# Layer scores as 64x64 products on the band of keys that each half block of queries sees

## The reference

```
h = shift_token(x);  q, k, v = split(h @ wqkv)         # 8 heads of 64
q, k = rotary_xpos(l2norm(q) * qs, l2norm(k) * ks)
# blocks of 128 queries, which see their own block of keys and the one before it
sim = q . k   masked where  i < j  or  i > j + 128
x = x + (softmax(sim) @ v) @ wo
h = layernorm(shift_token(x));  a, g = split(h @ w1 + b1)
x = x + (a * gelu(g)) @ w2 + b2
```

## Time and profile before

| | us |
|---|---|
| median of 3 runs | 1422.95 |
| lowest and highest run | 1420.28, 1424.81 |
| the profiled execution's own time | 1424.29 |
| its span, first to last instruction | 1422.5 |

### The profile page before, as it was taken

How to read it: one execution, slowest core, us unless ns; L and a number is a source line. 1 busy time by engine, 2 the same in 40 slices (tenths; PEclk the granted TensorE clock), 3 DMA queues, 4 the chain that set the end, 5 groups by cost and what they waited for, 6 DMA issues and landing times.

```text
span 1422.5 us, 24115 instructions
## 1 busy us (share of the span) xinstructions
PE 1374.8 (97%) x7740; PEld 1050.5 (74%) x7740; DVE 963.8 (68%) x2671; ACT 878.1 (62%) x2223; POOL 762.1 (54%) x522
## 2 busy tenths in 40 slices
PE   6999997999999999999999999999999999999988
PEld 5878775777777777777777777786777777777756
DVE  6877765767676666666667777676767676766657
ACT  4556656575747575747475766666565757575763
POOL 2425765564647373738373747464655646473710
PEclk9999999999999999999999999999999999999998
DMA  7111100000000000000001010000000000000046
GB/s 220 38 51 60 55 30 1 1 1 0 0 0 0 0 0 0 0 0 0 0 1 60 14 47 1 1 0 0 0 0 0 0 0 0 0 0 0 0 145 210
DMA packets 35243, 33.33 MB, mean 23 GB/s; under 512 B 8364, under 2 KB 32896, under 8 KB 35200
## 3 DMA queue, kind: packets, MB, share of 16 engines
q1 hardware_dynamic: 35200, 32.79, 7.3%
HBM read 24.39 MB, written 8.39 MB: 23 GB/s over the span
## 4 chain that ended last, share of the span: by engine, by line
PE 78%; ACT 11%; DVE 5%; issue 4%; POOL 1%; DMA 0%; ACTq 0%; SPq 0%; DVEq 0%; POOLq 0%
PE l_psF L1399 9%; PE l_psP L842 9%; PE l_ring L842 9%; PE l_ring L1399 8%; PE l_ring L1469 7%; ACT l_att L1073 7%; PE l_psP L1453 6%; PE l_psF L1487 6%; PE l_psS L1410 5%; PE l_psS L1422 4%; PE l_ring L653 3%; PE l_psF L1439 2%; PE l_psS L671 1%; PE l_psP L688 1%; ACT L1163 1%
## 5 line engine op out<-in xcount | busy, mean ns | idle before, releaser
L955 POOL TENSOR_TENSOR l_att<-l_att 128x1024 f32<-128x1024 f32 x64 | 153.1, 2403 | 315.7 <-DVE l_att L880 315.7
L1007 POOL TENSOR_TENSOR l_att<-l_att,l_rinv 128x1024 f32<-128x1024 f32 x64 | 126.4, 1975 | 70.7 <-DVE l_rinv L1243 70.4
L1053 ACT ACTIVATE l_att<-l_psP 128x384 f32<-128x384 f32 (+1 forms) x128 | 70.3, 549 | 120.7 <-PE l_psP L1453 120.4
L1248 DVE COPY l_att<-l_psP 128x384 f32<-128x384 f32 (+1 forms) x128 | 78.9, 617 | 86.7 <-PE l_psP L1453 82.5
L1453 PE MATMUL l_psP<-ident,l_att 128*128 128x128 f32 x896 | 124.5, 279 | 2.0 <-DVE l_att L1248 1.5
L1453 PEld LDWEIGHTS l_psP<-ident,l_att 128*128 128x128 f32 x896 | 98.6, 141 | 32.4 <-issue 28.2
L962 POOL TENSOR_TENSOR l_att<-l_att,l_rn 128x1024 f32<-128x1024 f32 x64 | 120.8, 1910 | 0.7 <-ACT l_rn L861 0.5
L1073 ACT ACTIVATE l_att<-l_psF,l_nb 128x256 f32<-128x256 f32 x256 | 118.1, 483 | 2.1 <-DVE l_nb L1236 2.1
L971 POOL TENSOR_TENSOR l_u_lo<-l_att,l_u_hi 128x512 fp32r<-128x512 f32 x75 | 95.7, 1288 | 39.1 <-ACT l_u_hi L1048 39.0
L1469 PE MATMUL l_ring<-l_att 128*64 128x256 f32 (+1 forms) x1024 | 112.5, 362 | 2.0 <-ACT l_att L1053 1.4
L1236 DVE CUSTOM_DVE_ANT_0 l_psF<-l_psF,w_mask 128x256 f32<-128x256 f32 x256 | 101.1, 456 | 16.3 <-issue 16.3
(11 more groups left out here) (209 smaller groups left out, 4037.2 us busy)
## 6 DMA issues: line engine op xcount, KB each, us to landing
a_tables<-in_x SPq DMA_DIRECT2D x8, 512.0 KB, 4.3
scratch_s<-a_o SPq DMA_DIRECT2D x8, 512.0 KB, 3.2
l_att<-in_x SPq DMA_DIRECT2D x8, 512.0 KB, 8.8
l_att<-scratch_s SPq DMA_DIRECT2D x8, 512.0 KB, 9.0
out_dram<-l_att SPq DMA_DIRECT2D x7, 512.0 KB, 7.8
aw_stage<-in_wqkv SPq DMA_DIRECT2D x2, 768.0 KB, 5.9
l_att<-in_wqkv SPq DMA_DIRECT2D x2, 768.0 KB, 5.4
w_w_raw<-in_w SPq DMA_DIRECT2D x2, 640.0 KB
```

The source lines that it names most:

```text
L955: pool.tensor_tensor(rot[:, t, :], rot[:, t, :], t2[t % 2], ALU.add).then_inc(S["added"], 1)
L1007: pool.tensor_tensor(pr, pr, along(inv, 2 * P), ALU.mult).then_inc(S["p_done"], 1)
```

## The change

`scores` makes of each product of 128 queries and 256 keys two products of 64 queries and 192 keys (`part` 0 and 1, whose results go to partitions 0 to 63 and 64 to 127). The four products of a block (two heads, two halves) use the four 64x64 quarters of the array. The first block of all has 128 keys for both halves. In the steps with both halves, unit 1 keeps the two products of its first block whole (`scores(i, 1, 1)`).

The waits of `scores` become a function of their own, `score_operands`. In the steps with both halves it is called with `ahead` from the group that comes before the scores: from `hidden`'s last tile ahead of the last product (and, because the loop passes there twice, also ahead of its low part), from `down` ahead of the last product of the four tiles (for unit 2) and of the fifth tile (for unit 3), and from `p_transposes` of units 0 to 3 ahead of the last transpose (for units 4 to 7). In the first step the waits stay in front of the scores.

```diff
+BAND = P // 2
...
-        def hidden(i, j, attn, parts=("hi", "lo")):
+        def hidden(i, j, attn, parts=("hi", "lo"), ahead=None):
...
                     for n, (k, w, a) in enumerate(terms):
+                        if ahead is not None and n == 3 * KD - 1:
+                            score_operands(i, ahead)
...
-        def down(i, c, tiles):
+        def down(i, c, tiles, ahead=None):
...
                 for m, (w, u) in enumerate(((W.w2_hi, U_hi), (W.w2_hi, U_lo), (W.w2_lo, U_hi))):
+                    if ahead is not None and k == tiles[-1] and m == 2:
+                        score_operands(i, ahead)
...
-        def scores(i, u, tiles=0):
+        def score_operands(i, u, tiles=TT):
+
+            if u < 2:
+                ge(pe, S["qT_sb"], TT * i + tiles)
+                ge(pe, S["kT_sb"], TT * i + tiles)
+            else:
+                ge(pe, S["exp_done"], UNITS * i + u - 1)
+
+        def scores(i, u, whole=0):
+
             pair, half = u // 2, u % 2
-            if u == 0 or tiles:
-                ge(pe, S["qT_sb"], TT * i + (tiles or TT))
-                ge(pe, S["kT_sb"], TT * i + (tiles or TT))
-            if u >= 2:
-                ge(pe, S["exp_done"], UNITS * i + u - 1)
             ps = scores_of[u % 2]
             for tt in range(2):
                 t = half * 2 + tt
-                c0 = 0 if t else P
                 for par in range(2):
                     rows = slice(par * DH, (par + 1) * DH)
-                    last = pe.matmul(ps[:, par * 512 + tt * 2 * P + c0:par * 512 + (tt + 1) * 2 * P], QT[rows, pair, t * P:(t + 1) * P],
-                                     KT[rows, pair, max(t - 1, 0) * P:(t + 1) * P], start=True, stop=True, skip_group_check=True)
+                    c = par * 512 + tt * 2 * P - (t - 1) * P
+                    for part in range(1 if tt < whole else 2):
+                        n = P if tt < whole else BAND
+                        q = t * P + part * BAND
+                        k0, k1 = (q - P, q + n) if t else (0, P)
+                        last = pe.matmul(ps[part * BAND:part * BAND + n, c + k0:c + k1], QT[rows, pair, q:q + n], KT[rows, pair, k0:k1],
+                                         start=True, stop=True, skip_group_check=True)
...
-        def p_transposes(i, u):
+        def p_transposes(i, u, ahead=None):
...
                     for own in (range(2) if u % 2 or tt else (1,)):
+                        if ahead is not None and par and tt and own:
+                            score_operands(i, ahead)
...
-                    hidden(i, j, attn)
+                    hidden(i, j, attn, ahead=0 if attn and j == HT - 1 else None)
...
-                    scores(i, 0, TT - 1)
+                    score_operands(i, 0, TT - 1)
+                    scores(i, 0)
...
             if attn and ffn:
                 scores(i, 0)
                 ge(pe, S["u_done"], HT * (i - 1) + HFULL)
+                scores(i, 1, 1)
+            elif attn:
+                score_operands(i, 1)
                 scores(i, 1)
-            elif attn:
-                scores(i, 1, TT)
...
-                down(i, 0, range(0, 4))
+                down(i, 0, range(0, 4), ahead=2 if attn else None)
...
                     if u < UNITS:
+                        if not ffn:
+                            score_operands(i, u)
                         scores(i, u)
                     if ffn and u in (2, 4):
-                        down(i, 0, range(3 + u // 2, 4 + u // 2))
+                        down(i, 0, range(3 + u // 2, 4 + u // 2), ahead=u + 1 if u == 2 else None)
...
                     if u >= 3:
-                        p_transposes(i, u - 3)
+                        p_transposes(i, u - 3, u + 1 if ffn and u + 1 < UNITS else None)
```

## The result

The changed kernel takes 1427.13 us (median of 14 runs, 1425.41 to 1429.21). The kernel before takes 1422.59 us beside it (14 runs, 1420.28 to 1425.93). The ratio is 1.0031, with a 95% interval of 1.0023 to 1.0040: slower by about 0.3%. The forecast was 1425.2 us and a ratio of about 1.0016, with 1423 to 1430 as its own range. So the direction is as forecast, and the size is about twice the forecast's. The profiled execution has a span of 1426.2 us (1422.5 before).

A forecast was written before the change was run, and what follows sets the result against it. TensorE is busy 97%, but the scores stretch was taken as bound by a chain of ScalarE's exponentials, last transposes, copies and values. 15 x 0.18 - 0.5 = +2.2 us on 1422.95 gave 1425.2 us, range 1423 to 1430.

The forecast's parts named there:

- four side by side at the quarter rate: Scores units: four quarter products run at once, 0.41 ns a column; psF 0.26 us and psS 0.16 us shorter.
- Rival B: Scores products: the four don't run side by side; +3.3 us an iteration, 1472 us; chance 0.10.
- the estimate by the Trainium skill: Scores units: issue costs some 62 ns a matmul, 1.14 us a unit, +1.5 us an iteration, 1445 us; chance 0.03.
- the moved wait holds the last product, and through it both copies: Unit 4's wait in unit 0's transposes: the last transpose waits, and ScalarE's copy starts 0.41 us later.
- Rival A: Moved waits hold nothing back and the shorter units count: -0.59 us an iteration, 1413.6 us; chance 0.17.
- nothing is gained by moving them: Entries to the scores: moved waits shorten no entry, gain taken as 0; ends 0 and 0.20 us at six entries.
- the last term: After unit 3's transposes: VectorE's copy takes 0.66 us, values group starts at 682.77 instead of 682.59; +0.18 us an iteration.
- no scores product lies on the chain that is left: Chain from unit 2's exponentials to the last values group: it holds no scores product; the iteration grows by 0.18 us.
- shorter scores only fill waits: Steps with both halves: the shorter scores products give nothing on the chain; the iteration grows by 0.18 us.
- First step: Attention half alone, no moved waits: shorter units give 0 to 1.7 us, taken as 0.5 us less.
- "Same": Whole kernel: time within 0.3%, 4.3 us, of the kernel before; chance 0.55.
- "slower": Whole kernel: slower by more than 0.3%, from above +0.29 us an iteration; chance 0.28.

The follow-up runs named there:

- e2: The changed kernel with its waits moved but the scores products as before the change: ratio 1.0066 to the kernel before.
- e5: The changed kernel with the waits of units 5 to 7 back in front of their scores, unit 4's still ahead of the last transpose: ratio 0.9974 to before.
- e6: The changed kernel with the waits of units 4 to 6 back in front of their scores, unit 7's still ahead of the last transpose: ratio 0.9985 to before.
- e9: e1 with the waits on the scores products themselves and TensorE's loop over the steps written out: ratio 0.9956 to the kernel before.
- e1: The changed kernel with quarter products kept and all waits back in front of the scores, on instructions of their own: ratio 0.9956 to the kernel before.
- e10: e8 with the waits on the scores products themselves and TensorE's loop written out: 1413.33 us, ratio 0.9937 to the kernel before.
- e8: e1 with the sixth second-layer tile placed after unit 0's transposes, before scores 4, instead of after scores 4: 1413.25 us, ratio 0.9926 to the kernel before.
- e13: The kernel before, whole scores products, with only the sixth second-layer tile moved behind unit 0's transposes: ratio 0.9993 to the kernel before.

## Why the forecast was right in kind and small in size

Step by step, from scores 0, forecast against the changed kernel's step 6:

| | forecast | measured |
|---|---|---|
| psF unit, psS unit | 0.81, 0.70 | 0.81, 0.71 |
| first `down` product | 1.80 | 1.83 |
| scores 2, 3 | 4.96, 6.79 | 4.97, 6.79 |
| ScalarE's copy of unit 0 | 8.84 | 8.83 |
| scores 4, 5 | 8.73, 11.47 | 8.72, 11.45 |
| values after scores 5 | 12.32 | 12.36 |
| scores 6, 7 | 14.79, 17.53 | 14.82, 17.56 |
| VectorE's last copy | 17.64 | 17.67 |
| values after scores 7 | 18.35 | 18.51 |
| growth of the period | 0.18 | 0.33 |

**Right: four side by side at the quarter rate.** Within a psF unit the trace has the products start in fours, 7 ns apart (673.100, .107, .113, .120), and each four 0.162 us after the one before. These are 768 columns in one of the two passes, so two passes cost 0.42 ns a column; I had taken 0.41. Rival B falls. So does the estimate by the Trainium skill (TensorE: Matmul & The Clock Gate, "Wait — 56ns, not 53.3ns?"): four instructions in 0.162 us are 41 ns each, less than its 62. (The prediction's 1.14 us for such a unit is also added up too low: 16 x 0.062 and its fixed part of 0.18 are 1.17.)

**Right: the moved wait holds the last product, and through it both copies.** Copy of unit 0 0.40 us later against scores 0 (0.41 said), a wait inside the transposes of unit 3 of 0.71 us, ended by exponentials (nearly 1 said: these transposes began 0.15 us later than forecast, which the wait covers; more on this below). Rival A's premise, that they hold nothing, is refuted by e2, e5 and e6; its arithmetic for a kernel in which they don't is right to 0.08 us (e9).

**Right: nothing is gained by moving them.** Entries whose wait was satisfied long before are no shorter: the transposes of unit 2 up to scores 6 take 0.81 us with the moved wait (680.11 to 680.92) and 0.80 without, and scores 3 last 0.81 us to the next start in the changed kernel, in e1 and in e9. The change of shape is what costs. Inside unit 1 no wait stands between whole and quarter products, and yet the first quarter starts 0.306 us after the last whole product, where 256 columns take 0.216 within the unit of before. The weight loads show it too (changed kernel, start, length):

```profile
666.80 0.30 PEld L1452 LDWEIGHTS l_psF<-l_att 64*128 64x128 f32 x4 [0.28 <-issue]
667.43 0.21 PEld L1452 LDWEIGHTS l_psF<-l_att 64*64 64x64 f32 x8 [0.33 <-issue]
667.91 0.19 PEld L1415 LDWEIGHTS l_ring<-l_u_hi,w_w_hi 128*128 128x128 f32 x1 [0.28 <-issue]
```

The load begins only with the first product of the new shape, never a product ahead as in the earlier trace rows. The rule of the Trainium skill (TensorEngine Tiling (Array Packing), Key Properties) is that a change of tiling mode drains TensorE; these rows agree with it, with 0.09 us more at the change of shape.

**Mis-sized: the last term, "VectorE's copy starts at 682.06 and takes 0.66: 682.72, and the values group starts at 682.77".** The copy came 0.03 late, and then 0.84 us stand where I had 0.71. The copy took 0.69, as the other one in the earlier trace rows had; and from its end (683.76 + 0.69 = 684.45) to the first value product (684.60) 0.15 us pass, where I took 0.05. My 0.05 was read from ScalarE to TensorE. The row before could not show VectorE's: there the values began when scores 7 let them (681.53 + 1.06 = 682.59), 0.33 us after the copy's end. The runs give VectorE's price. It is 0.145 to 0.146 us at the values group after scores 7 in four kernels (the changed one, e6, e9 and e10), though scores 7 start between 16.65 and 17.56 in them, and 0.15 again at unit 1's transposes in e8, e10 and e13. In the changed kernel it stands in one more place: the copy of unit 2 ends at 15.49, and unit 3's transposes start at 15.64. The profile puts the scores and not the copy on the chain in front of the values; but scores 7 last 0.95 us to the next start there (683.65 to 684.60), and 0.81 where no copy is late. Why VectorE's release is longer than ScalarE's no run settles. The 0.03 + 0.13 are the 0.16 between forecast and result in this stretch. In the period they are 0.15 (0.33 against 0.18), over 15 iterations 2.3 us. That is the miss as far as the medians tell: the kernel grew by 4.5 us between them (1427.13 - 1422.59), and by 3.7 between the two profiled spans, where I had 2.2. One of the periods, that of step 8 after the change of layers, grew by 0.13 and not by 0.33.

**Too strong: "no scores product lies on the chain that is left", "shorter scores only fill waits".** Scores 5 and 7 of the changed kernel would let the values start only 0.09 and 0.14 us before the copy beside them does. e2 shows what the shorter products are worth with the waits moved, 0.30 us an iteration, and e1 what without, 0.41. The sum had this in it, since it took the copy's path where that ended last; the sentence did not.

**First step:** 76.94 us before, 76.56 after, where I took 0.5 less. TensorE's granted clock is at its lower level (0.5, 1.2 GHz) in part of this step in every profiled execution but that of e2, and the step lasts between 74.51 us (e2) and 77.01 (e13). So the 0.38 is not shown to be the edit's.

On the odds: 1.0031 lies on the border of 0.3%, with the interval on both sides of it. (The prediction puts that border at +0.29 an iteration; with its own 0.5 us less in the first step it is +0.32.) "Same" at 0.55 and "slower" at 0.28 hold it together; the run doesn't decide between them.

## What to carry to other kernels

A wait on an in-order engine holds all that stands behind it. Before a wait is taken early, ask which semaphore the next instruction raises, and who waits for it: here two copies, and through them the exponentials, hung on the one product that the wait was put before. Two edits in one change should be timed apart: the products gave 0.41 us an iteration and the waits took 0.63, and together they looked like a small loss. And a wait for another engine (0.41 us before scores 4) is a place for independent work, which gave 0.20 us an iteration, where putting the waits on the products themselves gave 0.10.

## What the runs showed of the hardware that was not expected

- Four f32 products of 64 rows and 64 columns go side by side: 7 ns between their starts, 0.162 us for 192 columns.
- A change from products of 64x128 to products of 64x64 costs time as well (0.306 us from start to start where 0.216 is usual), though the rows are the same.
- The release of a waiting TensorE product has no one price. After ScalarE's exponentials it is 0.05 us when the product carries the wait (scores 4 and 7 in e9), and 0.145 when an instruction of its own in TensorE's stream carries it (the same in e1). After VectorE's copy it is 0.15 us at the values group after scores 7 (the changed kernel, e6, e9, e10) and at transposes (e8, e10, e13), but 0.10 at the values group after scores 5 (the changed kernel, e1, e9). Why the last two differ is not shown.
